# The order of work around the starts of two quantized FFNs, in a kernel of attention projection, FFN, Mamba-2 mixer and FFN

## The reference

```python
x = x + attn_a(layernorm(x), mask, weight, bias)   # dense, 32 x 32 blocks of the weight masked
x = x + ffn(layernorm(x), ...)
x = x + mixer(layernorm(x), ...)                   # in_proj, conv, scan over chunks, gate, norm, out_proj
x = x + ffn(layernorm(x), ...)                     # the same weights again

def ffn(x):                                        # 512 -> 1792 -> 512, weights are int32 with groups of 128
    gate, up, down = dequantize(gate_w), dequantize(up_w), dequantize(down_w)   # (w - zero) * scale
    return (silu(x @ gate) * (x @ up)) @ down
```

## Time and profile before

| | us |
|---|---|
| median of three runs (lowest, highest) | 2160.95 (2159.29, 2161.57) |
| the profiled execution, its own time | 2160.95 |
| its span, first to last instruction | 2159.2 |
| PE busy | 2109.3 |
| DVE busy | 1671.8 |
| ACT busy | 1399.5 |
| POOL busy | 916.1 |

### The profile page before, as it was taken

One profiled execution on the slowest core, in us unless ns is written; L12 is line 12 of the kernel. 1 busy time (PEld: TensorE's weight loads), 2 busy tenths in 40 slices (PEclk: granted clock), 3 DMA queues, 4 the chain that ended last, 5 costly groups with the idle time before them and its releaser, 6 DMA issues.

```text
span 2159.2 us, 37467 instructions
## 1 busy us (share of the span) xinstructions
PE 2109.3 (98%) x13386; PEld 1734.5 (80%) x13386; DVE 1671.8 (77%) x2682; ACT 1399.5 (65%) x1901; POOL 916.1 (42%) x622
## 2 busy tenths in 40 slices
PE   7999988999999999999999999999999999989999
PEld 6788866788888888888888888888888888877887
DVE  7555467978888888888787888888887878875554
ACT  5322247877777877777777877777777778752221
POOL 1222124555454545454554545554544545432221
PEclk9999989999999999999999999999999999999999
DMA  5544224332333333333323333333333233354441
GB/s 200 162 145 139 70 65 126 114 101 96 110 96 98 110 100 116 95 102 109 99 98 108 100 99 116 104 118 98 99 102 109 91 111 99 110 180 160 140 146 39
DMA packets 128645, 241.89 MB, mean 112 GB/s; under 512 B 14049, under 2 KB 48609, under 8 KB 128225
## 3 DMA queue, kind: packets, MB, share of 16 engines
q1 hardware_dynamic: 128480, 239.73, 35.2%
HBM read 234.17 MB, written 5.51 MB: 111 GB/s over the span
## 4 chain that ended last, share of the span: by engine, by line
PE 80%; DVE 3%; issue 2%; ACT 2%; POOL 0%; DMA 0%; SPq 0%; DVEq 0%; POOLq 0%; ACTq 0%
PE ring L958 35%; PE ring L1058 15%; PE bank_e L406 6%; PE yt L1039 6%; PE st L1023 4%; PE yt L1045 4%; PE bank_e L417 3%; PE xt L1010 3%; PE arg L996 2%; PE xt L971 1%; PE arg L1088 0%; PE st L983 0%; DVE xc L1378 0%; DVE m_xn L1489 0%; DVE f_gu_f L255 0%
## 5 line engine op out<-in xcount | busy, mean ns | idle before, releaser
L958 PE MATMUL ring<-m_lnt,w_sb 128*128 128x512 f32 x3456 | 859.8, 399 | 1.9 <-DVE xc L1378 1.9
L958 PEld LDWEIGHTS ring<-m_lnt,w_sb 128*128 128x128 f32 x3456 | 631.8, 189 | 129.5 <-DVE xc L1378 2.1
L1642 POOL TENSOR_TENSOR w_sb<-w_raw,w_sb 128x512 fp32r<-128x512 f32 x288 | 430.8, 1501 | 132.2 <-ACT w_sb L1201 131.9
L1657 POOL TENSOR_TENSOR ysq<-ysq,y 128x512 f32<-128x512 f32 x126 | 163.5, 1298 | 662.3 <-ACT y L1245 662.3
L1058 PE MATMUL ring<-wo,ygs 128*128 128x512 f32 x1536 | 369.7, 390 | 2.0 <-issue 2.0
L1058 PEld LDWEIGHTS ring<-wo,ygs 128*128 128x128 f32 x1536 | 287.1, 188 | 63.6 <-issue 2.7
L1378 DVE SCALAR_TENSOR_TENSOR xc<-ring,cw,xc 128x511 f32<-128x511 f32 (+2 forms) x384 | 286.2, 745 | 23.2 <-ACT xc L1213 14.1
L1647 POOL TENSOR_TENSOR wo<-wo_raw,wo 128x512 fp32r<-128x512 f32 x128 | 220.1, 1720 | 0.0
L1201 ACT ACTIVATE w_sb<-w_raw 128x512 fp32r<-128x512 f32 x288 | 177.2, 620 | 52.3 <-DMA w_raw<-w_in 52.3
L1213 ACT ACTIVATE xc<-ring,cb,cw 128x512 f32<-128x512 f32 x128 | 99.1, 774 | 149.4 <-PE ring L958 149.4
L1039 PE MATMUL yt<-em,x_dt 128*64 128x128 f32 x2048 | 184.0, 279 | 5.8 <-DVE state L1420 5.8
(11 more groups left out here) (199 smaller groups left out, 3142.1 us busy)
## 6 DMA issues: line engine op xcount, KB each, us to landing
w_raw<-w_in SPq DMA_DIRECT2D x288, 256.0 KB, 4.0
ce<-e_t SPq DMA_DIRECT2D x128, 384.0 KB, 4.1
wo_raw<-w_out SPq DMA_DIRECT2D x128, 256.0 KB, 4.4
f_gu_q<-gu_w SPq DMA_DIRECT2D x28, 512.0 KB, 3.7
f_gu_zr<-gu_z SPq DMA_DIRECT2D x28, 512.0 KB, 4.5
f_gu_sr<-gu_s SPq DMA_DIRECT2D x28, 512.0 KB, 5.3
f_dn_q<-dn_w SPq DMA_DIRECT2D x28, 256.0 KB, 3.6
f_dn_zr<-dn_z SPq DMA_DIRECT2D x28, 256.0 KB, 4.1
```

The source lines that it names most:

```text
L958: mm = nc.tensor.matmul(dst[:], w_sb[:, u % WR, wp, k * P:(k + 1) * P], lnt[:, xp, k, b * S:(b + 1) * S], start=(i == 0), stop=(i == 3 * K ...
L1642: nc.gpsimd.tensor_tensor(w_sb[:, u % WR, 1], w_raw[:, u % NR], w_sb[:, u % WR, 0].bitcast(F32), ALU.subtract).then_inc(w_lo, 1)
L1657: nc.gpsimd.tensor_tensor(part, part, y[:, k % 2], ALU.add).then_inc(ysq_done, 1)
```

## The change

Five orders are changed; no operation is added or left out.

1. In pair 0 of both FFNs, DVE and ACT take `deq_gu(1, 0)` and `high_gu(1, 0)` before `hidden(0, 1, 0)`, as in the other pairs, and no longer after it.
2. On PE, the turns of tiles 6 and 7 come between unit 0 and unit 1 (`tensor_between`), and no longer after eight of unit 0's twelve up matmuls (`tensor_in_up`). In the first FFN the turns of tiles 4 and 5 come between gate and up of unit 0 (`tensor_middle`), where those of the second FFN stood already, and no longer before gate.
3. In both leads `high_gu(0, 1)` comes before the high copies of tiles 6 and 7 on ACT. In the mixer's lead DVE's `deq_gu(0, 1)` stands between the lows of 5 and 6, whole, where its subtraction stood ahead of the lows of 4 to 7 and its scaling behind them; and the highs of 4 and 5 come before the centring of 6 and 7.
4. In the mixer, `high_gu(0, 0)` moves ahead of `y_high` of step K, and `scale_gu(0, 0)` from step K + 1 to the place after the accumulation of step K.
5. `wo` tiles 125, 126 and 127 are prepared one at step K - 1 and two at step K, instead of two and one, and their loads follow.

```diff
@@ -289,12 +289,9 @@
                         if not first:
                             hidden(p, 0, 0)
                             hidden(p, 0, 1)
-                        else:
-                            hidden(p, 1, 0)
                         if not last:
                             deq_gu(p + 1, 0)
-                        if not first:
-                            hidden(p, 1, 0)
+                        hidden(p, 1, 0)
                         hidden(p, 1, 1)
                         if not last:
                             deq_gu(p + 1, 1)
@@ -368,12 +365,9 @@
                         if not first:
                             hidden(p, 0, 0, first)
                             hidden(p, 0, 1, first)
-                        else:
-                            hidden(p, 1, 0, first)
                         if not last:
                             high_gu(p + 1, 0)
-                        if not first:
-                            hidden(p, 1, 0, first)
+                        hidden(p, 1, 0, first)
                         hidden(p, 1, 1, first)
                         if not last:
                             high_gu(p + 1, 1)
@@ -390,6 +384,8 @@
                         for j in range(2):
                             for half in range(2):
                                 u = 2 * j + half
+                                if first and u == 1:
+                                    lead.tensor_between(pe, n)
                                 if first and j == 0:
                                     pe.wait_ge(n.lo_done, (half + 1) * T // 2)
                                 if half == 0:
@@ -398,10 +394,8 @@
                                     pe.wait_ge(hf_done, 4 * p + (u - 1))
                                 for part, dst, done in ((0, g_bank, g_mm), (1, u_bank, u_mm)):
                                     if first and u == 0 and part == 1:
-                                        lead.tensor_up(pe, n)
+                                        lead.tensor_middle(pe, n)
                                     for i, (k, (a, b)) in enumerate((k, ab) for k in range(KT) for ab in PASSES):
-                                        if first and u == 0 and part == 1 and i == 2 * KT:
-                                            lead.tensor_in_up(pe, n)
                                         c = (part * KT + k) * P
                                         mm = nc.tensor.matmul(dst[half][:], gu[:, j, b, c:c + P],
                                                               lnt[:, a, k, half * TOK:(half + 1) * TOK],
@@ -637,8 +631,8 @@
                 high(n, 2)
                 norm_root(act, n, 3)
                 center(n, 3)
+                high_gu(0, 1)
                 high(n, 3)
-                high_gu(0, 1)
 
             def mix(self, pe, t):
                 pe.wait_ge(na.lo_done, t + 1)
@@ -678,14 +672,14 @@
                         norm_turn(pe, n, t)
                     self.mix(pe, 2 * i + 4)
                     self.mix(pe, 2 * i + 5)
+                pe.wait_ge(self.res, T - 3)
+
+            def tensor_middle(self, pe, n):
                 norm_turn(pe, n, 4)
                 norm_turn(pe, n, 5)
-                pe.wait_ge(self.res, T - 3)
-
-            def tensor_up(self, pe, n):
                 pe.wait_ge(self.res, T - 1)
 
-            def tensor_in_up(self, pe, n):
+            def tensor_between(self, pe, n):
                 norm_turn(pe, n, 6)
                 norm_turn(pe, n, 7)
                 pe.wait_ge(self.res, T)
@@ -867,7 +861,7 @@
 
         def wo_of(k):
 
-            return [k - 2] if 2 <= k < K - 1 else [K - 3, K - 2] if k == K - 1 else [K - 1] if k == K else []
+            return [k - 2] if 2 <= k < K else [K - 2, K - 1] if k == K else []
 
         class Mixer:
 
@@ -913,7 +907,7 @@
                 sp.dma_start(e_t, e_cum[:]).then_inc(e_stored, 16)
                 sp.wait_ge(parts_stored, 16 * 3)
                 load_args(0)
-                for k in range(K):
+                for k in range(K + 1):
                     if k > 0:
                         load_units(k + 1)
                     if k + 1 < K:
@@ -923,10 +917,8 @@
                         sp.wait_ge(prj_mm, NU)
                         sp.wait_ge(conv_done, len(CONVED))
                         tiles.load_gu(sp, 0, 0)
-                    if 1 <= k < K:
-                        load_out(k - 1 if k < K - 1 else K - 1)
-                    if k == K - 2:
-                        load_out(K - 2)
+                    if k >= 1:
+                        load_out(k - 1)
                     for t in range(CPB):
                         if k == END_AT - 4 + END_STEP * t:
                             need(sp, end_done, t)
@@ -1324,6 +1316,7 @@
                     if k == K:
                         norm_center_act(act, n, 0)
                         norm_center_act(act, n, 1)
+                        high_gu(0, 0)
                     if 0 < k < K - 1:
                         tap(("x", k + 1))
                     for unit in ahead[1:2]:
@@ -1347,7 +1340,6 @@
                     if k == K:
                         norm_high(act, n, 0)
                         norm_high(act, n, 1)
-                        high_gu(0, 0)
                         norm_center_act(act, n, 2)
                         norm_center_act(act, n, 3)
                     if k == K + 1:
@@ -1358,11 +1350,13 @@
                 norm_center_act(act, n, 4)
                 norm_center_act(act, n, 5)
                 norm_root(act, n, 3)
+                norm_high(act, n, 4)
+                norm_high(act, n, 5)
                 norm_center_act(act, n, 6)
                 norm_center_act(act, n, 7)
-                for t in range(4, T):
-                    norm_high(act, n, t)
                 high_gu(0, 1)
+                norm_high(act, n, 6)
+                norm_high(act, n, 7)
 
             def vector(self, dve, n, sub_gu, scale_gu, deq_gu):
                 def conv(unit):
@@ -1586,10 +1580,10 @@
                         factor_mean(1)
                     if 2 <= k <= K + 1:
                         y_low(k - 2)
-                    if k == K + 1:
-                        scale_gu(0, 0)
                     for i, t in out_tiles(k - 1):
                         accumulate(i, t)
+                    if k == K:
+                        scale_gu(0, 0)
                     if k == K + 4:
                         norm_inverse(dve, n, 2)
                         norm_shift(dve, n, 2)
@@ -1630,10 +1624,11 @@
                 end_pair(3)
                 norm_inverse(dve, n, 3)
                 norm_shift(dve, n, 3)
-                sub_gu(0, 1)
-                for t in range(4, T):
-                    norm_low(dve, n, t)
-                scale_gu(0, 1)
+                norm_low(dve, n, 4)
+                norm_low(dve, n, 5)
+                deq_gu(0, 1)
+                norm_low(dve, n, 6)
+                norm_low(dve, n, 7)
 
             def gpsimd(self, pool, n, low_gu):
                 def w_low(unit):
```

## The result

The changed kernel takes 2173.48 us (median of four runs, 2171.16 to 2173.67), the kernel before 2161.26: the ratio is 1.0057, 95% interval 1.0043 to 1.0073. The forecast was 2167.4, in a range that ended at 2170.4. So the sign was right, and the size half of what came: +12.2, not +6.5. The profiled execution took 2174.03, its span 2172.3, where the span before was 2159.2.

The account below looks back on a forecast made before the run. PE (TensorE), busy 98% of the span, was taken as the bound. Terms 2.94 + 2.0 - 1.6 - 2.0 = +1.3 of waiting plus 5.2 of clock gave +6.5: 2160.95 + 6.5 = 2167.4, range 2163.4 to 2170.4.

Parts of the forecast that it names:

- parts 1: Lead of the first FFN: later turns and highs of tiles 6 and 7 make PE restart 2.94 later.
- 2 (from turn 4 on): Lead of the second FFN, counted from turn 4: PE restarts 7.95 after it, +2.27.
- part 3: Pair 0 of both FFNs: down begins 19.6 after R, not 16.45; -1.6 and -2.0 before the new pause's clock.
- R: PE's restart after each FFN's lead, where 72 matmuls run without pause; forecast 59.41 in the first FFN, from 56.47.
- the two holds by GpSimd: Pair 0: GpSimd's low_dn delays DVE's deq_gu(1, 0) scaling, low_gu(1, 0) delays h_lo; without both, down begins at 18.2, not 19.6.
- (a): Rival: pauses come but the clock stays up after most; +1.3 to +4.3, 2162.3 to 2165.2; chance 0.18.
- all four FFN pauses: PE's new pauses: 3.2 and 3.5 in the leads, 3.0 before down in pair 0 of each FFN.
- (b): Rival: additions before down's fifth tile still late, 1.1 to 2 us more per FFN, up to 2172; chance 0.10.
- (c): Rival: down not held in pair 0, saving 4.8 and 5.2 there; 2159 in all; chance 0.06.
- the clock, 5.2 with bounds 0 and 6.7: Half clock behind the four FFN pauses: 1.5 each in the leads, 1.1 each before down, at most 1.68 each.
- the pause of 2.04: PE's old pause at 1903.5, at the mixer's end; forecast said no slow clock followed it.
- the balance of the mixer's end, -0.3 with bounds -0.5 and +0.2: Mixer's end: 0.4 gained at step K - 1, last yg_lo 0.3 later, waits around turns 2 and 3 gone; -0.3.

Follow-up runs that it names:

- the run with fillers: Changed kernel with idle matmuls, results overwritten, put into five pauses of PE (four in the FFNs, one at the mixer's end): 2164.67 us, ratio 1.0019.
- the first six experiments: Changed kernel with one part as before: mixer's end 2170.98, wo tiles 2173.40, scale_gu(0, 0) and high_gu(0, 0) 2172.79, lead highs 2167.06, PE's turns 2169.39, pair 0 2171.53.

## Why the prediction was wrong

**What held.** The steps of parts 1, 2 (from turn 4 on) and 3 measured what they said. R came 2.94 later in the first FFN and 2.31 in the second, for 2.94 and 2.27. In part 3 the two holds by GpSimd came as read from the earlier trace rows: in the changed kernel's pair 0,

```profile
75.04 2.20 DVE L255 TENSOR_TENSOR f_gu_f<-f_gu_q,f_gu_sr 128x1024 f32<-128x1024 f32 x1
...
80.30 1.00 DVE L279 TENSOR_TENSOR f_h<-f_hf,f_h 128x512 fp32r<-128x512 f32 x1 [0.70 <-ACT f_h L356]
```

with down 2.98 late, and no wait at its fifth tile. None of the rivals occurred: the clock fell behind all four FFN pauses, against (a), the additions were in time, against (b), and down was held, against (c). The splits by experiment (turns 2.1 of the first lead, order of the highs 1.7 in each) confirm the chain.

**The step that failed first: the clock, 5.2 with bounds 0 and 6.7.** In the profile its four pauses cost 1.55, 1.56, 1.58 and 3.0, which is 7.7, and the mixer's pause 2.4, together 10.1; the run with fillers got 9.6 of it back. Three things were wrong. The upper bound of 1.68 for one pause came from two rows with a slow stretch of some 3 us each; in the new kernel one of nearly 7 came too, at nearly twice the price. The two down pauses were discounted to 1.1 for being at the shortest that had been seen with half clock; one of them cost 1.56, the other 3.0. And the pause of 2.04 was taken for harmless from a single execution, and from a row that shows the pause and not the work behind it. In two later profiles the same pause was followed by half clock (12 products in 4.4 and 4.2, for 2.8), and only those of 1.7 or less in the leads had full clock behind them each time. How much of the 7.7 was this execution's luck can be told from the profiles of both kernels and of the first six experiments. They have 27 pauses of 2.9 to 3.4 us in the FFNs: 2 cost nothing, 17 cost 1.3 to 1.7, 8 cost 2.7 to 3.0, 1.8 on average. Four such pauses are 7.4, so that 5.2 was too little for the usual case, and the bound of 6.7 was not one.

**The step that failed as well: the balance of the mixer's end, -0.3 with bounds -0.5 and +0.2.** It was +3.3. Of that, 1.37 is the later last `yg_lo`, for 0.3. The forecast followed the port for `scale_gu` but not for `y_low(126)`, which stands two operations ahead: the `wo` subtraction straight behind GpSimd's sum of squares, which DVE had beaten by 0.26 before, came first by 0.02 and made `y_low(126)` 0.97 longer. The 1.37 is net of the 0.4 of step K - 1, which came: the products of `outputs(127)` start 22.65 after step K - 2 began, and before the change 23.07. The gains around turns 2 and 3 came too, 0.3 ahead of them and 0.3 between. The rest, 2.4, is clock, for which the forecast had no term here: it priced the four FFN pauses and left out the one that it had itself made longer.

**What is left open.** Why one pause is followed by a short slow stretch, another by a long one and a third by none is not settled: a pause of 2.04 had none or a short one, and pauses of 2.97 to 2.99 ahead of the same down matmuls had none, a short or a long one. It shows as a spread over equal runs: 2.5 us over the four of the changed kernel, 4.8 over 23 of the kernel before, 7.9 over the ten with the turns as before. How the 12.2 divides into parts is known within that spread only: single edits gave back 2.5 (mixer), 6.4 (highs), 4.1 (turns) and 2.0 (pair 0), which overlap, since a pause made shorter by either edit of the lead loses its clock price.

## What to carry to other kernels

A pause of TensorE has two prices, the wait and the half clock behind it; in the changed kernel's profile the five pauses stood for 16.3 of waiting and 10.1 of clock. Price every pause of 2 us or more with both, also one that is only made longer. Here a pause of about 3 us cost 1.8 of clock on average, between nothing and 3.0, so one profile does not tell its price. Before asking what a moved operation costs on its own engine, look for a GpSimd operation that reads SBUF and comes ready at the same moment as one of VectorE with both inputs there: the loser waited for all of it here, and two starts 0.02 apart could go either way. Work that another engine will want only a whole unit later (`deq_gu(1, 1)`) goes behind the additions that free the banks: that move was worth some 6.5 us.

## What was not expected of the hardware

- Half clock came in two sizes, or not at all. The granted clock was 0.56 over the seven us behind the changed kernel's last pause, against 0.72 over six us behind one of 3.2, and 1.00 behind pauses of 2.97 and 2.98 in two later runs. Behind the pause of 3.84 it was 0.50 in 1911.90 to 1917.10, having begun to fall inside the pause (0.85 in the window of it).
- A pause of 2.04 of otherwise unchanged work had a clock of 1.00 behind it in one execution and 0.61 in another.
- The table load of ScalarE ran ahead of its instruction's wait: it stood at 1913.98, right behind the centring, and the square root itself ran at 1918.50. In the kernel before, where the operand was there, the two were 1.30 apart. So it was no price on that path.

```profile
1913.98 1.28 ACT L1303 ACT_TABLE_LOAD   x1
1918.50 0.20 ACT L1303 ACTIVATE eps_row<-eps_row 128x4 f32<-128x4 f32 x1 [3.24 <-DVE eps_row L1536]
```

- Of two operations of VectorE and GpSimd that both read SBUF, the first one kept the other waiting to its end: 1.80 against 0.83 for the same operation of 512 elements. The Trainium skill's page SBUF — State Buffer says in its section "Who interferes with whom" that whoever issues first gets the shared pair for the whole instruction; the rows agree. With 0.02 between the two starts in the profile, GpSimd was first in five profiles and DVE in one, so the stamps do not settle so close a race.
